# Where stages of a transformer kernel meet: normalization on ScalarE, early transposes and early weight loads

## The reference

```
x = x + 0.5 * L0_ffn(_layernorm(x));  x = x + L0_attn(_layernorm(x));  x = x + 0.5 * L0_ffn(_layernorm(x))
... the same three for L1, L2 and L3; the order within a layer is always ffn, attn, ffn
_layernorm(x) = (x - mean) / sqrt(var + 1e-5)      over the 128 channels
```

## Time and profile before

| | |
|---|---|
| three runs | 3776.59, 3785.52, 3787.69 us (median 3785.52) |
| profiled execution | 3787.19 us, its span 3785.4 us |
| busy: PE, DVE, ACT, POOL | 88%, 70%, 50%, 28% of the span |
| mean granted TensorE clock | 0.921 |

### The profile page before, as it was taken

The page is one execution under the profiler, slowest core; times in us unless marked ns, Lnnn a source line. Parts: engine busy times, 40 slices in busy tenths (PEclk is TensorE's granted clock), DMA queues, the critical chain, the costliest instruction groups (busy, mean ns, idle before and its releaser), DMA issues. The chain is left out here.

```text
span 3785.4 us, 55832 instructions
## 1 busy us (share of the span) xinstructions
PE 3336.2 (88%) x21901; PEld 1709.0 (45%) x21909; DVE 2643.7 (70%) x5660; ACT 1901.5 (50%) x3422; POOL 1041.7 (28%) x832
## 2 busy tenths in 40 slices
PE   4678875899979999999889988888998898899899
PEld 3212234565633333333356665656775322332577
DVE  8787778777749999999377773454434777784433
ACT  2232222677756777777567772223223366766321
POOL 0344561867621000000096660001202111311100
PEclk9779977999988999999999998979999699999899
DMA  0000000311100000000021110001100000000100
GB/s 21 9 0 1 0 1 1 87 27 35 27 5 1 1 1 1 1 1 1 17 75 32 28 24 24 6 24 37 56 1 28 1 1 1 1 1 1 46 1 12
DMA packets 49631, 60.16 MB, mean 16 GB/s; under 512 B 9364, under 2 KB 34328, under 8 KB 49240
## 3 DMA queue, kind: packets, MB, share of 16 engines
q1 hardware_dynamic: 49368, 56.59, 5.4%
HBM read 39.22 MB, written 1.10 MB: 11 GB/s over the span
## 5 line engine op out<-in xcount | busy, mean ns | idle before, releaser
L142 PE MATMUL ps<-AR 128*128 128x128 f32 (+8 forms) x16848 | 2137.9, 434 | 152.1 <-DVE AR L114 36.7
L131 ACT ACTIVATE AR<-ps 128x512 f32<-128x512 f32 (+6 forms) x1808 | 1279.9, 748 | 1130.9 <-PE ps L142 856.2
L142 PEld LDWEIGHTS ps<-AR 128*128 128x128 f32 (+5 forms) x16848 | 1029.6, 152 | 1288.0 <-DVE AR L125 393.1
L125 DVE TENSOR_REDUCE AR<-ps 128x1 f32<-128x512 f32 (+1 forms) x1424 | 935.8, 708 | 117.1 <-PE ps L142 116.5
L114 POOL TENSOR_TENSOR AR<-AR 128x512 f32<-128x512 f32 (+5 forms) x486 | 622.0, 1293 | 793.9 <-ACT AR L131 553.0
L131 ACT ACTIVATE AR<-ps,AR 128x128 f32<-128x128 f32 (+2 forms) x700 | 355.8, 526 | 320.2 <-PE ps L142 292.5
L114 POOL TENSOR_TENSOR rs<-rs,halves 128x4 f32<-128x4 f32 x64 | 67.9, 1062 | 1495.1 <-DVE rs L118 1494.3
L142 PE MATMUL ps<-XT,AR 128*128 128x512 f32 x896 | 439.1, 626 | 20.3 <-DMA AR<-in_L3f_w 8.4
L114 DVE TENSOR_TENSOR AR<-ps,AR 128x512 f32<-128x512 f32 (+3 forms) x626 | 299.1, 527 | 131.1 <-PE ps L142 90.4
L122 DVE SCALAR_TENSOR_TENSOR X<-ps,AR,X 128x128 f32<-128x128 f32 x512 | 143.6, 343 | 339.9 <-PE ps L142 339.7
L150 PE MATMUL ps<-C,AR 128*128 128x128 f32 (+1 forms) x1593 | 249.2, 292 | 109.1 <-DVE AR L114 46.9
(11 more groups left out here) (82 smaller groups left out, 1766.8 us busy)
## 6 DMA issues: line engine op xcount, KB each, us to landing
AR<-AR SPq DMA_DIRECT2D x124, 128.0 KB, 2.3
AR<-in_c_rot SPq DMA_DIRECT2D x64, 128.0 KB, 2.2
AR<-in_L3f_w SPq DMA_DIRECT2D x32, 256.0 KB, 5.8
AR<-in_L2f_w SPq DMA_DIRECT2D x32, 128.0 KB, 2.9
AR<-scr_bias SPq DMA_DIRECT2D x32, 128.0 KB, 3.1
WR<-in_c_rot SPq DMA_DIRECT2D x4, 512.0 KB, 5.9
WR<-in_L_ffn_wqkv SPq DMA_DIRECT2D x2, 768.0 KB, 5.4
AR<-in_L_ffn_wqkv SPq DMA_DIRECT2D x2, 768.0 KB
```

Of the source, the lines that this page charges most:

```text
L125: return self.do(lambda e: e.tensor_reduce(o, a, AXX, op, negate=neg, apply_absolute_value=mag), *w)
L131: return self.do(lambda e: e.activation(o, a, f, bias=bias, scale=scale, accum_out=acc), *w)
L142: last = e.matmul(o, l, r, start=a, stop=z, skip_group_check=True)
```

## The change

1. `centred` makes `nm = -mean * rs` with one DVE instruction of 128x4 and normalizes with four ACT instructions (`Identity`, scale `rs`, bias `nm`). Chunk 3 is still normalized by DVE behind the barrier.
2. `turn_ahead` turns chunks 0 to 2 at the end of the stage, ahead of the barrier, where the next stage is not `l0_ffn` or `l1_ffn` (8 of 11 seams); `turn` and `turn_in` leave those out.
3. `fetch_ahead` issues first loads of the next stage at the end of S's queue of this one: `WQ` and `QS` of `l1_ffn`, all seven of `l2_attn`, the router and the first expert's `W1` of the mixtures. `l0_attn`, `l1_attn` and `l3_attn` get none. `moe_down` now waits for `W2` itself.
4. In `l3_attn` alone, `HI` is a plain ACT copy, `QK` is made by POOL (`G.ts`), and `MQK` by DVE (`V.stt`) in place of POOL.

```diff
@@ build
             stage(g)
+            if not g.last and stages[k + 1] not in (l0_ffn, l1_ffn):
+                turn_ahead(g)
+            if not g.last:
+                fetch_ahead(g, stages[k + 1])
             barrier(g)
+def fetch_ahead(g, stage):
+    S, I, wr = g.S, g.I, g.wr
+    g.d_ah = g.d_two[(g.d_ah is g.d_two[0]) * 1]
+    if stage is l1_ffn:
+        wr.at = 2152
+        g.wq0, g.qs0 = wr.f32(1536), [wr.f32(4, 64) for _ in range(2)]
+        for l in range(2):
+            g.t_ahead = g.d_ah.load(S, g.qs0[l], I["h_qs"][l])
+        g.t_ahead = g.d_ah.load(S, g.wq0, I["L1_ffn_wqkv"][0])
+    elif stage in (l2_ffn, l3_ffn):
+        wr.at, n, pre = (1714, 256, "L2f_") if stage is l2_ffn else (3664, 512, "L3f_")
+        g.w10, g.wrt = wr.f32(n), wr.f32(8)
+        g.d_ah.load(S, g.w10, I[pre + "w1"][:, 0, :], g.t_turn)
+        g.t_ahead = g.d_ah.load(S, g.wrt, I[pre + "wr"])
+    elif stage is l2_attn:
...
@@ settled, centred
-    t = statistics(g, x[0:4], c, *w)
+    t = statistics(g, [g.X[:, 4 * c + k, :] for k in range(4)], c, *w)
     centred(g)
-    g.waiting.append((c, x, t))
+    g.waiting.append((c, t, w))
     while g.waiting:
-        c, x, t = g.waiting.pop(0)
-        g.early[c] = center(g, x[0:4], x[4:8], c, t)
+        c, t, w = g.waiting.pop(0)
+        i = slice(4 * c, 4 * c + 4)
+        t = g.V.stt(g.nm[:, i], g.mv[:, i, 0], -1.0, g.rs[:, i], ALU.mult, ALU.mult, t)
+        g.early[c] = [g.A.act(g.XN[:, k, :], g.X[:, k, :], ACT.Identity, t, *w, scale=g.rs[:, k:k + 1], bias=g.nm[:, k:k + 1])
+                      for k in range(4 * c, 4 * c + 4)]
+def turn_ahead(g):
+    for n, c in enumerate(sorted(g.early)):
+        b = n % 2
+        t = g.P.tr([(g.bank[b][:, 128 * k:128 * k + 128], g.XN[:, 4 * c + k, :]) for k in range(4)],
+                   g.ident, g.early[c], g.free[b])
+        g.free[b] = g.turned[c] = g.A.act(g.XT[:, 512 * c:512 * c + 512], g.bank[b], ACT.Copy, t)
@@ turn, turn_in
+        if c in g.turned:
+            out.append(g.turned.pop(c))
+            continue
@@ l1_ffn
-    twq = g.d_r.load(S, wts[0]["WQ"], I["L1_ffn_wqkv"][0])
+    twq = tqs = g.t_ahead
@@ attn8: spread, spread_low
-        thi = A.act(HI[:, x, :], RAW[:, x, :], ACT.Copy, traw, tw, scale=MK[:, 1 + k:2 + k])
+        thi = A.act(HI[:, x, :], RAW[:, x, :], ACT.Copy, traw, tw, scale=1.0 if causal else MK[:, 1 + k:2 + k])
-        if not k:
+        if causal:
+            tqk = G.ts(QK[:, k, s, cols], RAW[:, x, :], MK[:, 0:1], MK[:, 3:4] if k else None, ALU.mult,
+                       ALU.add if k else None, traw, tw, skf[s])
+        elif not k:
...
-        t = G.tt(MQK[:, k, s, cols], HI[:, x, :], RAW[:, x, :], ALU.add, thi)
+        if causal:
+            t = V.stt(MQK[:, k, s, cols], HI[:, x, :], MK[:, 1 + k:2 + k], RAW[:, x, :], ALU.mult, ALU.add, thi, tw)
+        else:
+            t = G.tt(MQK[:, k, s, cols], HI[:, x, :], RAW[:, x, :], ALU.add, thi)
@@ moe
-            t = P.mm([(g.bank[b], W1[:, e, 128 * m1:128 * m1 + 128], g.XT[:, 512 * c:512 * c + 512], True, True)],
-                     g.free[b], tex[e], *w)
+            t = P.mm([(g.bank[b], W1[e][:, 128 * m1:128 * m1 + 128], g.XT[:, 512 * c:512 * c + 512], True, True)],
+                     g.free[b], tex[e] if e else tah, *w)
```

More of the change, by code:

```diff
@@ L223, in build @@
         g.half = sb("halves", 16)
+        g.nm = sb("nm", 16)
         g.wr = Arena(sb("WR", 4200), 4200)
@@ L229, in build @@
         g.free = [None] * 8
-        g.early, g.waiting, g.out, g.last = {}, [], out, False
+        g.early, g.waiting, g.turned, g.out, g.last = {}, [], {}, out, False
         g.near_bias = None
+        g.t_turn = None
+        g.d_two = [DmaSem(sem("d_ah%d" % i)) for i in range(2)]
+        g.d_ah = g.d_two[0]
         V, A, G, P, S = (Queue(sem(n)) for n in ("s_dve", "s_act", "s_pool", "s_pe", "s_sp"))
@@ L287, in build @@
         assert max(q.count for q in (V, A, G, P, S)) < 60000
+def fetch_ahead(g, stage):
[13 more added lines that the diff above has]
+    elif stage is l2_attn:
+        wr.at = 2152
+        g.l2w = wr.f32(4, 128), wr.f32(2), wr.f32(3, 128), wr.f32(NT, 2)
+        for k, n in enumerate(("wq", "wk", "wv", "wo")):
+            g.d_ah.load(S, g.l2w[0][:, k, :], I["L2a_" + n])
+        g.d_ah.load(S, g.l2w[1], I["L2a_bq"])
+        g.d_ah.load(S, g.l2w[2], I["L2a_bb"])
+        g.t_ahead = g.d_ah.load(S, g.l2w[3], I["c_sc"])
 def barrier(g):
@@ L320, in settled @@
         return
-    x = [a[:, 4 * c + k, :] for a in (g.X, g.XN) for k in range(4)]
-    t = statistics(g, x[0:4], c, *w)
+    t = statistics(g, [g.X[:, 4 * c + k, :] for k in range(4)], c, *w)
     centred(g)
-    g.waiting.append((c, x, t))
+    g.waiting.append((c, t, w))
 def centred(g):
     while g.waiting:
-        c, x, t = g.waiting.pop(0)
-        g.early[c] = center(g, x[0:4], x[4:8], c, t)
+        c, t, w = g.waiting.pop(0)
[9 more added lines that the diff above has]
+        g.free[b] = g.turned[c] = g.A.act(g.XT[:, 512 * c:512 * c + 512], g.bank[b], ACT.Copy, t)
 def normalize(g, src, dst, *w):
     if g.waiting:
-        centred(g)
+        c, t, _ = g.waiting.pop()
+        x = [a[:, 4 * c + k, :] for a in (g.X, g.XN) for k in range(4)]
         early, g.early = g.early, {}
+        early[c] = center(g, x[0:4], x[4:8], c, t)
         return sum((early[c] for c in range(4)), [])
@@ L841, in l1_ffn @@
         m = g.wr if l == 0 else ar
[L842 to L845, removed]
-    twq = g.d_r.load(S, wts[0]["WQ"], I["L1_ffn_wqkv"][0])
+        wts.append(dict(WQ=ar.f32(1536) if l else g.wq0, WO=m.f32(4, 128), W1=m.f32(682), W2=m.f32(3, 128), B1=m.f32(6), LG=m.f32(2),
+                        B2=m.f32(128), QS=g.qs0[l]))
+    assert g.wr.at <= 1714
+    twq = tqs = g.t_ahead
     tqs = [V.ts(w["QS"][:, 0:2, :], w["QS"][:, 0:2, :], 8.0, None, ALU.mult, None, tqs) for w in wts][-1]
@@ L1224, in l1_ffn @@
     st.emit()
+    g.free[0] = g.free[1] = [tok["top", 1, 15], tok["exp1", 1, 15]]
 def attn8(g, pre, names, scale, causal):
@@ L1620, in attn8 @@
     value_step(*steps[-1])
+    g.t_turn = list(trc.values()) if causal else None
     if fin_due:
@@ L1647, in l2_attn @@
     I = g.I
[L1648 to L1656, removed]
+    W, bq, bb, sc = g.l2w
+    tw = g.t_ahead
     QT = ar.f32(2048)
@@ L1781, in moe @@
     pre = "L2f_" if top2 else "L3f_"
-    W1 = ar.f32(8, nf * 128)
+    W1 = ar.f32(7, nf * 128)
+    W1 = [g.w10] + [W1[:, e, :] for e in range(7)]
     W2 = ar.f32(8, nf, 128)
-    WR = ar.f32(8)
+    WR = g.wrt
+    tah = g.t_ahead
     BR = ar.f32(8)
     LT = ar.f32(2, 8, 8)
-    g.d_w.load(S, WR, I[pre + "wr"])
     g.d_w.load(S, BR, I[pre + "br"]) if not top2 else None
@@ L1798, in moe @@
         d = (g.d_ms + g.d_ps)[e]
-        d.load(S, W1[:, e, :], I[pre + "w1"][:, e, :])
+        if e:
+            d.load(S, W1[e], I[pre + "w1"][:, e, :])
         tex.append(d.load(S, W2[:, e, :, :], I[pre + "w2"][:, e, :, :]))
@@ L1830, in turn_in @@
         b = 4 + c % 2
+        if c in g.turned:
+            return g.turned.pop(c)
         t = P.tr([(g.bank[b][:, 128 * k:128 * k + 128], g.XN[:, 4 * c + k, :]) for k in range(4)],
@@ L1837, in logits @@
         return P.mm([(g.bank[6][:, 8 * i:8 * i + 8], g.XT[:, 128 * i:128 * i + 128], WR, True, True) for i in range(NT)],
-                    tT, tw, g.free[6])
+                    tT, tah, g.free[6])
     tT = [turn_in(0), turn_in(1)]
@@ L1906, in moe @@
             if len(todo) > 1:
-                moe_down(g, todo.pop(0), HT, W2, L2, nf, hf, tg, txs)
+                moe_down(g, todo.pop(0), HT, W2, L2, nf, hf, tg, txs, tex)
             if bias_steps and 3 <= e < 7:
@@ L1913, in moe, with moe_down @@
                 gate_add(*gates.pop(0))
-    moe_down(g, todo.pop(0), HT, W2, L2, nf, hf, tg, txs)
-def moe_down(g, what, HT, W2, L2, nf, hf, tg, txs):
+    moe_down(g, todo.pop(0), HT, W2, L2, nf, hf, tg, txs, tex)
+def moe_down(g, what, HT, W2, L2, nf, hf, tg, txs, tex):
     e, c, th = what
@@ L1924, in moe_down @@
                           W2[:, e, m1, :], m1 == 0, m1 == nf - 1))
-    t = g.P.mm(parts, th, g.free[b])
+    t = g.P.mm(parts, th, g.free[b], tex[e])
     for m1 in range(nf):
```

2 lines of the change are left out of this document (removed).

## The result

The changed kernel takes 3808.01 us (median of five runs, 3805.95 to 3813.99) against 3785.52 in the same comparison: a ratio of 1.0068, interval [1.0053, 1.0084]. It is slower, by 0.68%; the forecast was 3785 and its range ended at 3801. The profiled execution after took 3808.01 us, its span is 3806.2, 20.8 more than before, and its mean granted clock 0.918.

A forecast was written before the change was run, and what follows sets the result against it. PE, busy 88% of the span, was taken as the bound, so seam changes save only PE's standing. Seams +0.7 and `l3_attn` -1.1 gave -0.4 us against 3787.19: 3785 us on the median's scale, range 3769 to 3801.

The forecast's parts named there:

- Prices: Centring on ACT: four instructions take 1.5 us, and making and handing over `nm` 0.25 us.
- The way to the barrier: Stage ends: barriers come 0.4 us later at three seams and 2.7 at the eight with early turning, +22.8 us.
- The 2.3 for the turning: At the eight turned seams: two ACT copies and PE's turning of chunk 2 add 2.3 us ahead of the barrier.
- Work queued behind the waiting ACT: Inside stages, work behind ACT's centring comes later: +6.4 us for two `l0_ffn`, +1.3 for `l0_attn`, +8 for two `l1_ffn`.
- My 2.65 for that chain: End of the first `l0_ffn`: from ACT's first copy to the last product takes 2.65 us.
- The rival in which ACT's order costs double: Each late chunk is charged again as PE cools and resumes at half rate: +15.7 becomes +31, 3800 us; chance 0.05.
- What is saved: Attention ends and stage starts: -5.6 DVE centring, -19.6 mixtures' first matmul, -6.6 `l1_ffn`, -2.8 `l2_attn`, -3.2 router.
- `l3_attn`: New pieces there: head -2.0, loops +3.9, clock -3, sum -1.1 us (-14 to +15).
- the -3 that I had put for it: Behind the head of `l3_attn`: without PE's stand the clock may fall later or less, -3 us.
- that rival: The head of `l3_attn` keeps its clock: -15 us in place of -3, 3773 us in all; chance 0.20.
- The rule on two SBUF inputs: In `l3_attn`, DVE's new two-input add would stand behind POOL's instruction on a shared port; the sum has no such term.

The follow-up runs named there:

- its reverse: The changed kernel with all centring back on DVE, early turning, early loads and new `l3_attn` pieces kept: 3778.04 us, ratio 0.9984 to the kernel before.

## Why the prediction was wrong

By its own steps, on the profiled scale: -0.4 us was forecast and +20.8 came.

- **Prices: near.** The group of four ACT centrings takes 1.65 us, 1.5 was taken; `nm` is handed over 0.19 us behind its start, 0.25 was taken. One instruction has 477 to 494 ns. The Trainium skill, ScalarE: Activation LUTs, section What ACT_TABLE_LOAD costs, gives a fixed cost, a cost for each element, one for each operand from SBUF and the overlap of neighbours; the estimate by them is 479 ns for one and 1.64 for four, and the trace agrees.
- **The way to the barrier: right.** The eight turned seams are 2.5 to 2.97 longer and the three others 0.59: 24.6 us in all against 22.8. The 2.3 for the turning stood a little above its own parts, 2.17 at the lower clock, and that came out near.
- **Work queued behind the waiting ACT: the step that failed.** Each delay of ACT was forecast within half a microsecond (gates +1.2, copies at 109.3, DVE's product +2.35), but I added delays only. PE stood while ACT was late and came back at a lower granted clock, or had it fall just behind, and in the end of `l0_ffn` copies and products alternate, so the low clock is paid along the whole chain: 6.59 us where it was 4.46. My 2.65 for that chain was wrong even without the clock, since the earlier trace rows show 4.46; X of chunk 3 came 7.1 us later and not 3. Within the stages, without their barriers, `l0_ffn` has +7.1 and +8.1 for +3.2 each; `l1_ffn`, between its first and its last statistics, +3.9 and +8.1 for +4 each; `l0_attn` +2.2 for +1.3; and each `l2_ffn` +2.0, where the Gelus behind a centring were left out. That is 33 for 15.7. Of these 18 us the lower clock has 4.6 in the two `l0_ffn` and the misread chain 3.6; the Gelus, wait and clock together, have 4; the rest is mostly in the second `l1_ffn`, where the parts were not separated. The rival in which ACT's order costs double had this mechanism, 3800 and a chance of 0.05. Part of its evidence stood in the earlier trace rows: a clock of 0.60 over the 59 us behind a stand of PE. It doesn't have the other two terms, so that its 3800 is near the result is in part luck. The kernel with ACT's centring alone and its reverse show the size, the one with `nm` early that half of it is the wait for DVE's statistics, at the barriers and inside the stages.
- **What is saved: right but for one seam.** `l1_ffn` starts its first matmul 3.5 and 3.6 us behind the barrier (forecast 3.7), the mixtures at it, and the first `l2_ffn` and the second `l3_ffn` gained about 1 us each more than forecast. In the first `l3_ffn` 6.8 were forecast and 0.7 came: I had read the wait that ended last in the row, the weight load, and not asked what the next instruction in PE's queue waits for, the bias table. The run with the table first shows it.
- **`l3_attn`: right within what can be told.** -1.1 was forecast, and two runs say 0.2 and 3.5 us for the pieces, which is within what the stage varies by. The clock behind the head stayed at 0.62, so the -3 that I had put for it is not seen. That activity releases the low clock, which I had cited for that rival from the Trainium skill (TensorE: Matmul & The Clock Gate, Part 1: The HAM clock gate), is not borne out in this head: PE is busy 49.7 of 59 us there and the clock is low for most of it; the row of 1.00 ahead of 0.60 shows only the fall behind a stand. The rule on two SBUF inputs that I cited from the Trainium skill (SBUF — State Buffer, section Who interferes with whom) was set beside a row that doesn't bear on it, a fill of POOL, which reads nothing from SBUF, and a centring with one tensor input. Of DVE's 32 new adds 29 take 0.74 or 0.75 us, several of them with a POOL instruction running all the while, and three take 0.91, 1.27 and 1.35: 1.3 us in all.

The sum of the first four: +1.8 for the barriers, +18 for the queues, +6 for the table, and some 4 taken back, 2.5 of them in `l1_attn` ahead of its end, with the clock told of below and so by luck, the others at the starts. That is the 21 us between forecast and result. That a late turning of chunk 2 stands ahead of eight barriers and pays only at a few was forecast in the sum, but as balanced by the gains of the loads; the runs with the loads alone and with two chunks turned show that loads and turning are separate, and that the same ideas, placed otherwise and with the table's loads ahead, are worth 0.9%.

## What to carry to other kernels

Moving an operation to an engine with room is priced by what stands behind it in that engine's queue and by what TensorE does in the gap: count the wait for its operands in full, and the products behind the gap at the lower clock. When a load is fetched early, walk on along the queues to the next operand that arrives late; small loads that are needed soon belong ahead of the large ones. Preparing the next stage ahead of a barrier costs nothing as long as the work is done within waits that are already there: with two chunks of three the barrier stayed within 0.1 us of its place.

## What was unexpected of the hardware

- **The clock after short stands.** All the stands that ACT's centring made and that were looked at were followed by the low clock, the short ones too: 1.95 us in `l2_ffn` (0.55 over the next 3.8 us), 2.04 in `l1_ffn` (0.83 over 10), 2.33 with `nm` early (1.00 until 1 us behind it, then 0.50) and 4.39 at the end of `l0_ffn` (0.58). Where the first products still ran at the full clock, as the six in 0.94 us, the fall came behind them; so the length of a row just behind a stand doesn't say what the stand costs.
- **The same work, other clocks.** In `l1_attn`, 80 to 130 us behind its barrier, the granted clock was 0.78 to 0.86 in the kernels of this study, though the stage's loops are the same in all. From the barrier to its first statistics, where at most the turning of chunks at the start differs, the stage took 788.8 us in the kernel with 0.86 and 796.3 in the one with 0.78, and the others lie between in the order of that clock. The end adds 9.2 us, or 7.8 with ACT's centring. What sets the clock there was not found. Single stages can't be compared more closely than some us; sums over paired runs can. The rows of two of them, the kernel before and the one with the early loads and the table first:

```profile
1165.10:1215.10 50.00, 48.35 (x301) 15.85 (x304) 45.35 (x76) 27.15 (x28) 0.00 (x0) 0.82 0.00 1
```

```profile
1155.80:1205.80 50.00, 48.48 (x290) 17.11 (x289) 46.29 (x81) 24.10 (x25) 0.00 (x0) 0.78 0.00 1
```

- **A fill on POOL stops one DVE instruction whole.** The view of the centring line in the kernel with two chunks turned (ns, min/median/max) shows a single instruction of 5.56 us among ones of 0.34, for as long as the 5.22 us fill ran; without the fill the group takes 1.16.

```profile
L119 DVE TENSOR_SCALAR XN<-X,mv,rs x6: 329/341/5556, 2610.3 to 2617.0; 128x128 f32<-128x128 f32 x6
```

  The Trainium skill, SBUF — State Buffer, section Who interferes with whom, says that DVE's `tensor_scalar` can use both of its port pairs, and that it and GpSimd then block each other for a whole instruction. The trace agrees, and it is this and not the one on two inputs that the row of 6.19 us in the earlier trace rows shows; the kernel's time did not change without the fill.
